# Four-layer graph network on one core: products of constants on TensorE ahead of its waits in the last group's layer 3 and in group 0's layer 0

## What is computed

```python
x = _layernorm(x + _L0_gnn_ref(x, adj, adj, W_q, W_k, W_v, W_e, W_o))  # masked attention, 8 heads
x = _layernorm(x + _L1_gnn_ref(x, adj, ...))                           # two convolutions, messages, GRU
x = _layernorm(x + _L2_gnn_ref(x, adj, W_w, W_b, a_w, a_b))            # weighted mean by exp(logits)
x = _layernorm(x + _L3_gnn_ref(x, adj, W, a))                          # attention, 4 heads:
    h = jnp.einsum('bni,io->bno', x, W).reshape(b, n, H, D).transpose(0, 2, 1, 3)
    e = e_i[:, :, :, None] + e_j[:, :, None, :]
    e = jnp.where(e > 0, e, LRELU_SLOPE * e)
    e = jnp.where(adj[:, None, :, :] > 0, e, NEG_INF)
    out = jnp.einsum('bhnm,bhmd->bhnd', jax.nn.softmax(e, axis=-1), h)
```

## Time and profile before

| quantity | value |
|---|---|
| median of 3 runs | 1408.46 us (1406.12 to 1408.89) |
| the profiled execution | 1408.24 us, its span 1406.5 us |
| PE busy in the span | 1344.6 us (96%) |
| DVE, ACT, POOL busy | 1212.4, 1185.0, 596.5 us |
| mean granted TensorE clock | 0.98 of full |

### The profile page before, as it was taken

One profiled execution on the slowest core, in us unless ns is written; L12 is line 12 of the kernel. 1 busy time (PEld: TensorE's weight loads), 2 busy tenths in 40 slices (PEclk: granted clock), 3 DMA queues, 4 the chain that ended last, 5 costly groups with the idle time before them and its releaser, 6 DMA issues.

```text
span 1406.5 us, 40636 instructions
## 1 busy us (share of the span) xinstructions
PE 1344.6 (96%) x13330; PEld 1043.0 (74%) x13330; DVE 1212.4 (86%) x3407; ACT 1185.0 (84%) x4450; POOL 596.5 (42%) x918
## 2 busy tenths in 40 slices
PE   6799999999999999999999999999999999999974
PEld 3577778877777877777787777787777778777753
DVE  7658889889999988999888999989898999888874
ACT  6877888988888998888898888889888888986664
POOL 1123444544344444435344434445443444545532
PEclk8999999999999999999999999999999999999995
DMA  3101010001011011101101101110110111000000
GB/s 134 31 31 32 31 32 31 17 32 39 16 40 39 25 38 39 32 24 39 39 24 39 40 17 38 39 39 24 39 39 17 39 39 32 24 17 31 9 16 24
DMA packets 23826, 46.88 MB, mean 33 GB/s; under 512 B 2753, under 2 KB 2754, under 8 KB 23490
## 3 DMA queue, kind: packets, MB, share of 16 engines
q1 hardware_dynamic: 23618, 44.27, 10.0%
HBM read 35.88 MB, written 8.39 MB: 31 GB/s over the span
## 4 chain that ended last, share of the span: by engine, by line
PE 89%; ACT 4%; DVE 4%; issue 2%; POOL 1%; DVEq 0%; POOLq 0%; ACTq 0%
PE B L708 18%; PE B L605 17%; PE B L508 14%; PE B L548 5%; PE B L572 4%; PE B L618 3%; PE B L519 2%; PE B L534 2%; PE B L761 2%; PE B L789 2%; PE B L662 2%; PE B L702 2%; PE B L827 2%; PE B L595 2%; PE B L773 2%; PE B L679 2%
## 5 line engine op out<-in xcount | busy, mean ns | idle before, releaser
L1019 ACT ACTIVATE e<-B,nm 128x128 f32<-128x128 f32 x1024 | 362.7, 384 | 12.8 <-DVE nm L1387 12.8
L508 PE MATMUL B<-ident,e 128*128 128x128 f32 x1536 | 233.5, 279 | 17.2 <-ACT pT L1028 8.8
L1377 DVE SCALAR_TENSOR_TENSOR B<-an,rowb,mask 128x512 f32<-128x512 f32 x256 | 190.6, 789 | 50.9 <-ACT h L1152 42.2
L1019 ACT ACTIVATION_READ_ACCUMULATOR e<-B,nm 128x1 f32 x1024 | 231.0, 226 | 0.0
L508 PEld LDWEIGHTS B<-ident,e 128*128 128x128 f32 x1536 | 178.8, 143 | 35.9 <-issue 12.3
L1177 ACT ACTIVATE e<-l,nm 128x128 f32<-128x128 f32 x512 | 198.7, 402 | 5.5 <-DVE nm L1616 5.5
L377 POOL TENSOR_TENSOR veps<-meanv,eps 128x4 f32<-128x4 f32 x128 | 26.4, 206 | 399.6 <-DVE meanv L1350 399.6
L1387 DVE TENSOR_REDUCE nm<-B 128x4 f32<-128x512 f32 x256 | 168.7, 673 | 26.2 <-PE B L548 26.0
L1028 ACT ACTIVATE pT<-B 128x512 f32<-128x512 f32 x256 | 155.6, 620 | 1.7 <-PE B L508 1.7
L380 POOL TENSOR_TENSOR rstd<-veps,neghalf 128x4 f32<-128x4 f32 x128 | 130.0, 1016 | 10.0
L391 POOL TENSOR_TENSOR xs<-xs 128x288 f32<-128x288 f32 x32 | 40.8, 1276 | 203.6 <-ACT xs L1059 203.6
(11 more groups left out here) (200 smaller groups left out, 3423.5 us busy)
## 6 DMA issues: line engine op xcount, KB each, us to landing
xt<-in_x_t SPq DMA_DIRECT2D x32, 256.0 KB, 3.4
an<-in_adj_n SPq DMA_DIRECT2D x32, 256.0 KB, 2.9
xn<-in_x_n SPq DMA_DIRECT2D x32, 256.0 KB, 3.0
at<-in_adj_t SPq DMA_DIRECT2D x32, 256.0 KB, 2.7
out_x<-xo SPq DMA_DIRECT2D x32, 256.0 KB, 3.3
wm<-in_mats SPq DMA_DIRECT2D x1, 1088.0 KB, 9.1
wm<-in_mats SPq DMA_DIRECT2D x1, 832.0 KB, 6.7
wm<-in_mats SPq DMA_DIRECT2D x1, 320.0 KB, 2.9
```

The source lines that it names most:

```text
L508: last = mm(g(dst, b), g(src, b), ident[:, :], is_transpose=True, start=(b == 0), stop=True, skip_group_check=True)
L1019: last = fn(g(e0[:, h % 2, :], b), g(bank, b), ACT.Exp, bias=nm0[:, h % 4, b:b + 1], accum_out=sum0[s % 2][:, b, head(h):head(h) + 1])
L1377: v.scalar_tensor_tensor(out=bank[:, :], in0=an[s % AN][:, :], scalar=we[:, head(h):head(h) + 1], in1=mask0[:, :], op0=ALU.mult, op1=ALU.a ...
```

## The change

A helper `keep_awake(s, n)` does nothing except in the last group (31), where it puts n products of `flat` into bank 1, behind a wait for the norm of layer 1 of that group, the last reader of the bank. It is called in six functions of layer 3: between the wait for the bank and the wait for the input in most, in `logits3` behind the wait for the mask, and in `values3` behind the waits for the bank and for `h3`. In layer 0 of group 0, `probs_T` for heads 2 to 7 gets two such products into its own bank, which the transposes overwrite. All results stay as they were.

```diff
+            def keep_awake(s, n):
+
+                if s < GROUPS - 1:
+                    return
+                pe.wait_ge(ln_out[1], GROUPS)
+                for _ in range(n):
+                    set_bank(1)
+
             def probs_T(s, h, bank, users):
                 freed(pe, s, users)
+                if s == 0 and h > 1:
+                    for _ in range(2):
+                        mm(bank[:, :], flat[:, :], flat[:, :].unsqueeze(1).broadcast_to([128, GB, N]), start=True, stop=True)
                 pe.wait_ge(q["exp_done"], H0 * s + h + 1)
                 transpose4(bank, e0[:, h % 2, :]).then_inc(q["tr_ps"], 1)
...
             def x3_T(s, bank, users):
                 freed(pe, s, users)
+                keep_awake(s, 8)
                 pe.wait_ge(ln_out[2], s + 1)
...
             def hidden3(s, bank, users):
                 freed(pe, s, users)
+                keep_awake(s, 4)
                 pe.wait_ge(q["x3T_ready"], s + 1)
...
             def logits3(s, banks):
                 pe.wait_ge(q["seed3_done"], GB * s + GB)
+                keep_awake(s, 12)
                 pe.wait_ge(q["ej_split"], s + 1)
...
             def probs3_T(s, b, bank, users):
                 freed(pe, s, users)
+                keep_awake(s, 4)
                 pe.wait_ge(q["exp3_done"], GB * s + b + 1)
...
             def values3(s, bank, users):
                 freed(pe, s, users)
                 pe.wait_ge(q["h3_ready"], s + 1)
+                keep_awake(s, 3)
                 pe.wait_ge(q["pT3_ready"], GB * s + GB)
...
             def out3_T(s, bank, users):
                 freed(pe, s, users)
+                keep_awake(s, 3)
                 pe.wait_ge(q["o3T_ready"], s + 1)
```

## The result

| kernel | median | lowest to highest | runs |
|---|---|---|---|
| before | 1408.92 us | 1406.12 to 1411.73 | 22 |
| changed | 1411.38 us | 1409.82 to 1414.71 | 22 |

The ratio is 1.0021 with a 95% interval of 1.0013 to 1.0028: slower, by 1.8 to 4 us. The median lies in the stated range (1407.0 to 1413.0). The loss of 2.5 us is 0.7 more than the forecast of 1.8, just beyond the 0.2% that I had set between "same" and "slower"; the interval lies on both sides of that limit.

The account below looks back on a forecast made before the run. TensorE's clock was taken as below full only at the run's two ends. Last group 1.2 us later plus 0.6 for a late clock rise, group 0 zero: 1408.46 + 1.8 = 1410.3 us, range 1407.0 to 1413.0.

Parts of the forecast that it names:

- The price of a product: One product on PE takes 0.42 us at half clock and 0.21 at full.
- The entry to layer 3: Products ahead of x3_T(31) and logits3: x3_T 0.2 us late, logits sooner; 0.5 us ahead at leaky(31, 0).
- on the way: Clock rises during the eight products ahead of x3_T(31), making it some 0.2 us late; otherwise 1.0 us late.
- the wait they stand in, before `x3_T(31)`, was 2.35 us: Empty PE wait ahead of x3_T(31), set against 3.4 us for eight products at half clock.
- Carried to the last step: From logits to the release of hidden3(31), only 0.1 us of the entry's 0.5 us gain is left.
- The last step: hidden3(31) release to values3 takes 7.35 us, 2.7 more; values3 gives back 0.9 and out3_T 0.5.
- half of 1.15 us: Last step, clock rising one piece later: hidden3 0.3 more, next four products 0.85 more; 0.6 us added.
- Group 0: Two products ahead of scores(0, 1) delay group 1 by 0.43 us; counted as even with a possible gain.
- The even chance of 0.98 back: scores(1, 0) at full clock instead of half would return 0.98 us; half of it was credited.
- Full clock to the end: Rival: clock stays full from x3_T(31) to the end, 0.6 us less than before, 1407.9 us; chance 0.2.
- Half clock throughout: Rival: products don't raise the clock, or only behind the last step; 8.6 us more, 1417 us; chance 0.1.
- The start gaining more than the end loses: Rival: scores(1, 0) and other first-slice pieces gain 1 us each, end even; 1406.5 us; chance 0.1.

Follow-up runs that it names:

- tail_only: Changed kernel with only the last group's 46 products, group 0 as before; 1.0018 of before.
- start_only: Changed kernel with only group 0's twelve products, the last group as before; 0.9999 of before.
- last_only: Changed kernel with only the last group's products from probs3_T(31, 1) on, none in group 0; 1.0020 of before.
- scores_only: Kernel before plus six products in bank 7 ahead of the seed wait of scores(1, 0), nothing in the last group; 1.0001 of before.
- head2_only: Changed kernel without last-group products; in group 0 eight products ahead of probs_T(0, 2) instead of two each for heads 2 to 7; 1.0012 of before.
- waits_only_2: The kernel waits_only run again on another chip call; 0.9981 of before.
- waits_only: Changed kernel, last-group products ahead of bank waits in hidden3, probs3_T, values3; none before probs3_T(31, 2), (31, 3) or in group 0; five before x3_T; 0.9989 of before.
- entry_only: Changed kernel with only the last group's products ahead of x3_T, logits3 and probs3_T(31, 0), none in group 0; 0.9993 of before.

## Why the prediction held, and which terms were off

**The price of a product** was right at both levels: twelve at full clock took 2.76 us, (2.76 - 0.39) / 11 = 0.215 each, and four at half 1.89, (1.89 - 0.63) / 3 = 0.42.

**The entry to layer 3** was mis-sized. I took `x3_T` 0.2 us late and the logits 0.5 early. Measured from the norm, `x3_T` was 1.5 us later than before in the changed kernel and 0.3 in tail_only, the logits 0.7 later and 0.5 earlier. Two steps failed in the changed kernel's trace. The first is that the clock rises "on the way": the eight products took 3.41 us and it rose only at their end, the case for which I had named 1.0 us late. The second is "the wait they stand in, before `x3_T(31)`, was 2.35 us": that length is of an execution in which `hidden3(30)` ran partly at full clock. In the changed kernel's it ran at half, PE was done with the transposes behind it only at 1371.65 + 1.06 = 1372.71, and up to 0.14 us behind the norm's end 1.5 us were left, 0.8 less. The eight products cost 3.05 us from there (to 1375.76), 0.3 less than the 3.4 of the sum. The four runs without products there say the same: start_only, last_only, scores_only and head2_only had a wait of 1.53 or 1.54 us. waits_only_2 with five products had `x3_T` 0.13 us behind its norm, waits_only 0.54.

**Carried to the last step**: I let 0.4 of the 0.5 us be lost between the logits and the release of `hidden3`. The stretch took 8.8 us where it was 9.0, so nothing was lost there and 0.2 gained: the products ahead of `probs3_T(31, 1)` began at full clock and took 1.43 us instead of 1.7, and the transposes behind them ended (1391.00) before ScalarE came to their copy (1391.20). With the entry, the release came 0.5 us later after the norm than before (17.7 against 17.2), where I had 0.1 earlier.

**The last step** was right in mechanism and in size: 7.35 us were forecast and 8.1 measured, but the sum also had 0.6 for a later rise of the clock, so 7.95. The clock rose in the four products behind `hidden3`, not in `hidden3`: 0.3 for that one, 0.4 for those four. That is the case for which I had added half of 1.15 us. `values3` and `out3_T` gave back 0.9 and 0.45, forecast 0.9 and 0.5.

That these 1.4 us are owed to the products is wrong, though. In entry_only, start_only, head2_only and scores_only, with no product in the last step, `values3` took 1.08 us too; this row is from start_only:

```profile
1397.91 1.08 PE L843 MATMUL B<-pT,h 128*32 128x128 f32 x32 [0.84 <-ACT pT L1203]
```

The trace of before, from which I took the half clock there, is again the odd one. From the end of the norm ahead of `x3_T(31)` to the end of the span it took 33.9 us; start_only, head2_only and scores_only took 32.6 or 32.7, tail_only with its full clock 33.3, the changed kernel 36.5, waits_only_2 30.0. Against the three, the products of the changed kernel cost 3.8 us in its profiled execution and 0.7 in tail_only's. A forecast of 1.8 lies between these two, and so does the measured 2.5, as the two groups of executions in the result do. That the number came so near is in part luck: a credit that belongs to no product, and a mixture of executions that I had not forecast. That the two groups are those in which the clock fell and those in which it stayed is my reading; only single executions were traced.

**Group 0**: 0.43 us forecast, and `scores(0, 0)` to `scores(1, 0)` grew from 22.78 to 23.16 us, 0.38; shown. The even chance of 0.98 back did not come in this trace. start_only is even with before within 0.1%, which fits the forecast of zero and can't tell it from 0.4 us.

**The rivals.** Full clock to the end happens, in tail_only's profiled execution, at the price its sum gave. The page of the Trainium skill "TensorE: Matmul & The Clock Gate", section "Why this matters for your kernels", has the clock fall in idle gaps between bursts of matmuls. The trace of the changed kernel does not quite follow a rule of gaps alone: with products in nearly all waits the clock fell at about 1389 us, behind waits of at most 1.51 us since 1378.7; in tail_only, with waits of at most 1.65 us there, it stayed. Half clock throughout did not happen in any trace. The start gaining more than the end loses was refuted by start_only and tail_only.

I gave "slower" 0.27 and "the same" 0.66. By the two traces the miss is in the entry (1.2 us too early), less the 0.6 that I had wrongly let the way to the last step lose, plus 0.2 in the last step: 2.6 us where the sum had 1.8. The remaining 1.5 us between the two spans were there already at the norm ahead of `x3_T(31)`; group 0 accounts for some 0.4 of them, the rest stays open.

## What to carry to other kernels

Work that is to keep an engine's clock up has a price like any other instruction: it must end before the wait that it stands in does. So put it ahead of the first wait of a piece and not between two waits: here the wait for the bank was the late one and the wait for the input long over. Pieces that ran back to back have no wait to fill; there a product cost its full length here, more than the clock gave back. How long a wait is differs with the clock of what runs ahead of it; leave room for half clock, and take the length from more than one execution.

## What I had not expected of the hardware

Executions of one kernel differ in where along the instructions the clock is full. waits_only and waits_only_2 are the same kernel. `scores(0, 0)`, the first large piece, took 1.17 us in the trace of waits_only_2, as in those of before and of the changed kernel, and 2.09 in that of waits_only:

```profile
11.81 2.09 PE L556 MATMUL B<-kh,qT 32*128 32x128 f32 x32 [0.78 <-DVE B L1392]
```

start_only took 2.09 as well, though it has the same instructions up to there as the changed kernel. Two to three such pieces, 1 us longer or shorter each, would by my estimate explain much of the 1406 to 1412 us over which before itself is spread, and they put a bound on what one trace tells about an effect of 1 us. And matmuls of nothing but ones help to hold the clock: from `x3_T(31)` to the end of the last step it was full for 23.5 us in waits_only_2 with products in the waits, where it was half for 20.9 us before without them.
